# TensorE's signals for the picks and the sums of a step: increments on the last matmul, or on a drain behind it

## The reference

```python
xn = _layernorm(x, axis=-1)
x = x + _L0_gnn_ref(xn, edge_index, ...) + _L0_mix_ref(xn[None], ...)[0]
x = x + _L0_ffn_ref(_layernorm(x, axis=-1)[None], ...)[0]
```

```python
h = (x @ W).reshape(N, H, C)                     # 4 heads of 64
e = jax.nn.leaky_relu(a_src[src] + a_dst[dst], negative_slope=NEG_SLOPE)
p = jnp.exp(e - m[dst])                          # m: maximum over a node's edges
denom = jax.ops.segment_sum(p, dst, num_segments=N)
out = jax.ops.segment_sum(alpha[:, :, None] * h[src], dst, num_segments=N)
```

## Time and profile before

| what | value |
|---|---|
| timed runs | 2243.01 us median of 3 (2241.64 to 2247.39) |
| profiled execution, first to last instruction | 2629.1 us |
| TensorE matmul / weight load busy | 1977.1 us (75%) / 1396.6 us (53%) |
| DVE, ACT, POOL busy | 1609.0 (61%), 1084.8 (41%), 1456.8 us (55%) |
| mean granted TensorE clock | 0.844 |

### The profile page before, as it was taken

One profiled execution on the slowest core, in us unless ns is written; L12 is line 12 of the kernel. 1 busy time (PEld: TensorE's weight loads), 2 busy tenths in 40 slices (PEclk: granted clock), 3 DMA queues, 4 the chain that ended last, 5 costly groups with the idle time before them and its releaser, 6 DMA issues. The chain is left out here.

```text
span 2629.1 us, 37526 instructions
## 1 busy us (share of the span) xinstructions
PE 1977.1 (75%) x9074; PEld 1396.6 (53%) x9075; DVE 1609.0 (61%) x3942; ACT 1084.8 (41%) x1932; POOL 1456.8 (55%) x1586
## 2 busy tenths in 40 slices
PE   8488887676766776766778777878888888898762
PEld 6365665554545554544555555555555666665431
DVE  7566666556666666586556665666765769553133
ACT  5322222234543443344545445555533655543110
POOL 3465656666666666655455555555565556530265
PEclk9788988887777777778888888898998998999876
DMA  9544544765555555545555555555556666531365
GB/s 319 142 133 132 141 123 116 221 185 143 160 153 144 156 151 148 151 129 148 147 167 158 149 153 142 150 149 146 146 152 165 163 166 160 155 109 59 116 194 168
DMA packets 286940, 401.66 MB, mean 153 GB/s; under 512 B 108852, under 2 KB 209492, under 8 KB 283199
## 3 DMA queue, kind: packets, MB, share of 16 engines
q0 software_dynamic: 74208, 206.08, 29.0%
q1 hardware_dynamic: 194348, 169.01, 21.9%
q10 hardware_dynamic: 18162, 24.08, 3.0%
HBM read 345.85 MB, written 81.96 MB: 163 GB/s over the span
## 5 line engine op out<-in xcount | busy, mean ns | idle before, releaser
L1534 POOL DMA_INDIRECT rows_g<-node_table,src_all x1347 | 1284.5, 954 | 922.1 <-issue 390.2
L2323 PE MATMUL psB<-rows_g,pick_e 128*128 128x260 f32 x2704 | 764.9, 441 | 111.7 <-issue 100.9
L2323 PEld LDWEIGHTS psB<-rows_g,pick_e 128*128 128x128 f32 x2704 | 589.6, 224 | 246.0 <-issue 141.7
L1709 DVE TENSOR_TENSOR rows_g<-rows_g,psD 128x2048 f32<-128x2048 f32 x169 | 384.9, 2277 | 0.0
L2122 ACT ACTIVATE pick_n<-local_row 128x1024 bf16<-128x1024 bf16 x169 | 178.6, 1057 | 389.6 <-remote 294.3
L1772 DVE COPY xn<-psD 128x256 f32<-128x256 f32 x112 | 47.4, 423 | 374.7 <-remote 143.7
L2364 PE MATMUL psC<-W_f,xnT 128*128 x448 | 246.3, 676 | 0.0
L2118 ACT ACTIVATE local_row<-local_row,minus_id 128x1024 bf16<-128x1024 bf16 x169 | 191.5, 1133 | 37.2 <-issue 25.2
L1680 DVE TENSOR_TENSOR pick_e<-psD,slot_all 128x1024 f32<-128x1024 f32 x169 | 203.8, 1206 | 0.1
L1556 POOL DMA_INDIRECT rows_g<-set_dram,places x98 | 96.2, 982 | 188.7 <-issue 165.3
L2312 PE MATMUL psA<-window,pick_n 128*128 128x24 bf16 x1352 | 61.2, 175 | 136.3 <-DVE psD L1690 49.8
(11 more groups left out here) (389 smaller groups left out, 3100.8 us busy)
## 6 DMA issues: line engine op xcount, KB each, us to landing
local_row<-local_dram SPq DMA_DIRECT2D x169, 256.0 KB
rows_g<-node_table,src_all POOLq DMA_INDIRECT x1347
xin<-sent_dram SPq DMA_DIRECT2D x112, 128.0 KB
set_dram<-xn SPq DMA_DIRECT2D x112, 128.0 KB
xnT<-in_xT_dram SPq DMA_DIRECT2D x96, 128.0 KB
sent_dram<-sorted_dram SPq DMA_DIRECT2D x96, 128.0 KB
sent_dram<-sorted_dram ACTq DMA_DIRECT2D x96, 128.0 KB
acc<-node_table SPq DMA_DIRECT2D x49, 128.0 KB
```

What stands on the lines that cost most here:

```text
L1534: pool.indirect_dma_start(out=rows_g[:, r, j], out_offset=None, in_=node_table, in_offset=bass.IndirectOffsetOnAxis(ap=src_all[:, g, j:j + ...
L1709: dve.tensor_tensor(heads, heads, p_here.unsqueeze(3).broadcast_to([P, EG, HEADS, C]), ALU.mult).then_inc(ph_ready, 1)
L2323: last = pe.matmul(ps_sum[s % 2][:, 0:AW], pick_e[:, s % SLOTS, j], rows_g[:, s % RING, j, 0:AW], start=(j == 0), stop=(j == EG - 1))
```

## The change

In `pick` and in `sums` the last matmul no longer carries an increment. Behind it stands a drain of TensorE, which carries the same increment of the same semaphore. The waits of the other engines, the order of all other instructions and the data are as before. There are 169 steps, so 338 drains.

```diff
--- before.py
+++ after.py
@@ -2309,9 +2309,9 @@
                     if s >= 2 and extras_until(s - 2):
                         pe.wait_ge(extra_kept, extras_until(s - 2))
                     for j in range(EG):
-                        last = pe.matmul(ps_pick[:, j * 6 * HEADS:(j + 1) * 6 * HEADS], pick_n[:, j * P:(j + 1) * P],
+                        pe.matmul(ps_pick[:, j * 6 * HEADS:(j + 1) * 6 * HEADS], pick_n[:, j * P:(j + 1) * P],
                                          window[:, w].rearrange("p k a -> p (k a)"), start=True, stop=True)
-                    last.then_inc(picked, 1)
+                    pe.drain().then_inc(picked, 1)
 
                 def sums(s):
                     pe.wait_ge(p_kept, s + 1)
@@ -2320,9 +2320,9 @@
                     if s >= 2:
                         pe.wait_ge(added, 2 * (s - 1))
                     for j in range(EG):
-                        last = pe.matmul(ps_sum[s % 2][:, 0:AW], pick_e[:, s % SLOTS, j], rows_g[:, s % RING, j, 0:AW],
+                        pe.matmul(ps_sum[s % 2][:, 0:AW], pick_e[:, s % SLOTS, j], rows_g[:, s % RING, j, 0:AW],
                                          start=(j == 0), stop=(j == EG - 1))
-                    last.then_inc(summed, 1)
+                    pe.drain().then_inc(summed, 1)
 
                 def turn_x(n):
                     u = n % 2
```

## The result

The changed kernel takes 2301.94 us (median of 4 runs, 2300.03 to 2306.37) where the kernel before took 2244.82 beside it: a ratio of 1.0258 with a 95% interval of 1.0243 to 1.0273, 57 us slower. The forecast was 2309, in a range of 2240 to 2358.

A forecast was written before the change was run, and what follows sets the result against it. TensorE has little slack in the first and third stages; GpSimd's gathers limit the middle. 287 drains at 0.42 us cost TensorE 120 us, of which 9 + 9 + 48 = 66 show: 2243 + 66 = 2309 us, range 2240 to 2358.

The forecast's parts named there:

- One drain on TensorE: Behind picks and sums: 0.15 us lost head start, 0.20 restart, 0.07 to 0.1 exposed weight load, together 0.42 us.
- The lower bound of 0.10 us: At line 2361, where the array empties by itself, emptying alone was read to cost 0.10 us.
- Places: Drains that cost TensorE time: 160 of 169 picks and 127 of 169 sums, 287 in all, 120 us.
- Share in the first stage: Key-values, 24 steps: half of the 0.71 us slip a step reaches the end, 9 us.
- Middle stage: Mixing, 60 steps: GpSimd's gathers set the pace, so a fifth of the slip shows, 9 us.
- Third stage: Expert blocks with routing, 85 steps: gathers wait for TensorE's picks, so 0.8 of the slip shows, 48 us.
- The signal: Increments of picks and sums come about 0.03 us later, which gathers and adds do not notice.
- What would show it: Signs: drain records 0.2 to 0.4 us, 0.3 us idle behind picks, TensorE busy unchanged, third-stage gather waits up.
- Absorbed: Rival, chance 0.14: the slip falls into the sums' waits for the vector engine; 2243 to 2249 us.
- Dearer drain: Rival, chance 0.12: a drain costs 0.73 us as sequencer work stands behind it; 115 us, 2358 us.
- Faster through late signals: Rival, chance 0.11: matmul increments arrive late and drains signal picks and sums earlier; 49 us less, 2194 us.
- the estimate of 28 us: Loss at the end if 287 drains cost the skill's 166 to 183 ns each, 50 us on TensorE.

The follow-up runs named there:

- e10: Kernel before, no drain: increments stay on the last matmuls and TensorE itself waits for each behind picks and sums; 2279.42 us, ratio 1.0166.
- e5: Kernel before plus one TensorE semaphore increment, not waited for, behind each pick and sums, no drain; 2248.11 us, ratio 1.0014.
- e12: Kernel before with drains behind picks and sums in steps 84 to 113 alone, the third stage's first 30; 2250.02 us, ratio 1.0036.
- e4: Kernel before with both drains added, but the increments left on the last matmuls; 2302.39 us, ratio 1.0259.
- e1: The kernel before once more, without an edit, for a second profile; 2245.21 us, ratio 0.9999.
- e2: Kernel before with drains carrying the increment behind the picks alone; 2266.35 us, ratio 1.0101.
- e3: Kernel before with drains carrying the increment behind the sums alone; 2274.03 us, ratio 1.0132.
- e11: Kernel before with five drains a step in steps 24 to 83 alone, three of them within the pick; 2248.10 us, ratio 1.0018.
- e8: Kernel before with drains behind picks and sums in steps 24 to 83 alone, the middle stage; 2247.98 us, ratio 1.0019.
- e6: Kernel before with two drains behind each pick and sums, the increment on the second; 2322.07 us, ratio 1.0346.

## Why the prediction was right, and where only the sum was

The direction and the mechanism held, and the sum came within 9 us (66 forecast, 57 measured). Its terms did less well, and that the sum came so near is partly luck: the first stage was put 9 us too low, the other two 15 too high.

- **One drain on TensorE: 0.42 us forecast, 0.38 to 0.40 measured at most places.** The lost head start was 0.15 to 0.16 as read. The restart was 0.23 instead of 0.20. The 0.07 to 0.1 for an exposed weight load is not there on top: line 2474's sixteen matmuls take 1.97 us behind a drain and 1.98 before. The load lies within the restart. The lower bound of 0.10 us for an emptied array, read at line 2361, was too low: e10 loses 0.21 to 0.22 at most places.
- **Places: 287 forecast, 319 measured.** I left out a quarter of the sums as covered by waits, by one group's idle time in the stretched trace. With the smaller price the product came out right, 120 against 117 us, because the two errors cancel.
- **Share in the first stage: a half, 9 us forecast, 18 (15 to 21) measured.** This term failed most. TensorE's 48 us without a matmul in the first 300 us of the long trace were stalls of that execution; in one of normal length there are 9 in 233. The 18 are more than the stage's 15 us of stops; the slower clock there may be the rest.
- **Middle stage: 9 us forecast, 4 measured,** and those no more than e5's without stops. The reason (gathers set the pace) was right, and it should have been priced at nothing.
- **Third stage: 48 us forecast, 38 (35 to 41) measured.** The gathers' waits for the picks were taken for a sign that TensorE comes last. e12 puts them mostly in the steps that lose least. The sign that held is the stretch's own balance: 25 us of 582 without a matmul. The growth was 0.42 to 0.45 us a step, a little under the 0.5 that was named as a sign.
- **The signal, 0.03 us later and unnoticed:** right in the main; it comes 0.034 us behind the modelled end instead of 0.014, and e4 has the drains without this delay and the same time.
- **What would show it:** idle before line 2474 appeared, at 0.23 us; line 2373 has it too. The two pages (busy, mean ns, idle before), the second profile of the unchanged kernel first:

```profile
L2373 PE MATMUL psC<-ident,hid 128*128 128x128 f32 (+1 forms) x546 | 92.2, 286 | 0.0
L2373 PE MATMUL psC<-ident,hid 128*128 128x128 f32 (+1 forms) x546 | 91.6, 285 | 11.1 <-issue 11.0
```

  GpSimd's waits grew in the third stage, and the middle one kept its length. Two signs were wrong: the drains' records last microseconds, not 0.2 to 0.4 us, and TensorE's matmul time rose by 52 us, most of it lost overlap, which is 46 us added place by place. By stage that overlap is 7, 18 and 21 us, and the matmul time rose by 15, 20 and 17, with a granted clock that fell in the first stage and rose from 0.95 to 0.96 in the third.
- **The rivals.** Absorbed: true of the middle stage alone. Dearer drain: the median gap behind a drain is 0.23 us, a stop of 0.38 to 0.40 and not of 0.73. Faster through late signals: fell with e1.

The Trainium skill, in "TensorE: Matmul & The Clock Gate", section "Single matmul latency", gives 166 to 183 ns as the constant that a single matmul pays besides its columns, and the estimate of 28 us was worked out from it. e10, which empties the array without a drain, loses 0.21 to 0.22 us a place, somewhat above that figure; the 0.17 that come with the drain are not in it, and the measured 0.38 to 0.40 decides. The Trainium skill's rule in "PSUM — Partial Sum Buffer", section "Engine vs sequencer instructions", to put the increment on the producing matmul and keep a drain for a standalone barrier, is given there for correctness; in this case keeping to it is also worth 57 us.

What stays open: why the two single kernels, e2 and e3, give 5 us less together than the change, which lies within their intervals; and why the middle stage is up to 6 us shorter in most of the traces whose first stage has drains (in e4's it is not); and what the 4 us of drains in the middle stage alone are, since e11's five stops a step cost no more than e8's two.

## What to carry to other kernels

Let the producing matmul carry the increment: a drain behind it empties TensorE, 0.2 to 0.4 us here each time the next matmuls were ready, the more where a wait instruction stands behind the drain. What such a stop costs at the end is read stage by stage from the time in which the engine has no matmul, in a profile whose span agrees with the timed runs: here all of it where there was next to none, and no more than a sequencer instruction's 3 to 4 us where another engine was back to back. That someone waits for an engine doesn't mean that it comes last; look at what that engine waits for itself.

## What the runs showed of the hardware that was not expected

- The restart behind a drain (0.229 and 0.234 us behind the modelled end) is four times that behind a wait for the same matmul's own increment (0.058 us). Of it 0.15 us are a separate wait instruction that is taken up only behind the drain; without one the restart is 0.08 us. A second drain on the emptied array has a record of 13 ns and puts the restart off by 0.077 us.
- One traced execution out of those here had 606 of 1176 of TensorE's increments late, and 386 us more than the timed runs, while nearly all increments of the vector engine and ScalarE that it recorded came on time (of the vector engine's it recorded only about half). It did not come again in a profile of the same kernel.
- In the first stage the granted clock is 0.98 before and 0.95 after, that is 11 us at 1.2 GHz instead of 2.4 in the one and 24 in the other. In the six normal traces without a stop there it is 11 to 17 us, in the five with stops at both places 21 to 41 (e6, with two drains, the 41). So the stops went with a slower clock there; what part of the 20 us is from it the traces bound, by up to 6.5 us, and don't tell.
